# A two-layer graph attention kernel: the order inside a software-pipelined step is rearranged

## The reference, cut to what matters

```python
h = relu(layernorm(x))
s = h @ W0 @ inp.T                         # only where adj > 0
x = x + softmax(s / 0.07) @ inp            # a row without ones: the mean of inp
h = relu(layernorm(x)) @ W1
e = leaky_relu(h @ a_src [rows] + h @ a_dst [columns])
att = softmax(e where adj > 0); att below 1e-4 is dropped, the rest times the row's count of ones
x = x + elu(h + att @ h)
```

## Time and profile before

| | us |
|---|---|
| median of 3 runs | 656.26 |
| the profiled execution | 656.63 |
| its span, first to last instruction | 654.8 |
| busy: DVE | 481.7 (74%) |
| busy: ACT | 408.3 (62%) |
| busy: PE | 399.8 (61%) |
| busy: POOL | 299.5 (46%) |
| mean granted TensorE clock | 0.81 |

### The profile page before, as it was taken

How to read it: one execution, slowest core, us unless ns; L and a number is a source line. 1 busy time by engine, 2 the same in 40 slices (tenths; PEclk the granted TensorE clock), 3 DMA queues, 4 the chain that set the end, 5 groups by cost and what they waited for, 6 DMA issues and landing times.

```text
span 654.8 us, 9849 instructions
## 1 busy us (share of the span) xinstructions
PE 399.8 (61%) x3012; PEld 274.8 (42%) x3043; DVE 481.7 (74%) x2172; ACT 408.3 (62%) x424; POOL 299.5 (46%) x335
## 2 busy tenths in 40 slices
PE   2465475767668696777677765866382521546654
PEld 0111233344436263544455443635271521546653
DVE  0176178798988798979898996979847413579994
ACT  3667778999999789979889979973221100022232
POOL 6001660515151332406076674747777767777000
PEclk9657577999998889978979998867856755657777
DMA  9999999999999999999999999942222232234222
GB/s 327 413 419 421 419 368 406 383 408 407 409 408 407 370 350 392 400 407 373 367 403 369 403 398 409 397 181 55 68 70 54 71 99 53 55 103 127 75 81 83
DMA packets 37767, 186.78 MB, mean 285 GB/s; under 512 B 7888, under 2 KB 8144, under 8 KB 18896
## 3 DMA queue, kind: packets, MB, share of 16 engines
q1 hardware_dynamic: 28496, 167.02, 64.8%
q0 software_dynamic: 9216, 19.11, 10.2%
HBM read 179.73 MB, written 6.37 MB: 284 GB/s over the span
## 4 chain that ended last, share of the span: by engine, by line
DVE 41%; DMA 14%; PE 12%; POOL 11%; issue 10%; ACT 10%; SPq 2%; DVEq 0%; ACTq 0%; POOLq 0%
DMA arena<-in_adj 13%; POOL arena L808 6%; ACT arena L862 6%; PE K L1424 4%; DVE keys L1018 3%; DVE G L1129 2%; ACT R_all L891 2%; POOL X L800 2%; DVE RTp L1188 2%; POOL arena L800 2%; DVE stats L1226 1%; POOL E L808 1%; PE G L1637 1%; DVE cand L1048 1%; DVE X L1368 1%
## 5 line engine op out<-in xcount | busy, mean ns | idle before, releaser
L862 ACT ACTIVATE arena<-arena,half_c 128x2048 fp8e4<-128x2048 int32 x144 | 283.7, 1999 | 38.0 <-DMA arena<-in_adj 35.9
L800 POOL DMA_INDIRECT X<-in_L_gnn_input,idx_all x132 | 125.8, 953 | 203.9 <-DVE idx_near L1100 167.0
L1424 PE MATMUL K<-arena,bits 128*128 128x512 fp8e4 x576 | 168.0, 431 | 47.4 <-DVE keys L1018 24.2
L808 POOL DMA_INDIRECT arena<-table,idx_near x96 | 92.5, 964 | 30.3 <-issue 29.0
L1424 PEld LDWEIGHTS K<-arena,bits 128*128 128x128 bf16 x576 | 58.9, 108 | 91.1 <-ACT arena L862 28.5
L1018 DVE MAX8 keys<-K 128x8 int32<-128x128 f32 x192 | 42.4, 281 | 41.4 <-PE K L1424 41.4
L808 POOL DMA_INDIRECT E<-table,idx_near x48 | 45.6, 949 | 14.6 <-issue 14.6
L1517 PE MATMUL W<-X,RTp 128*128 128x128 f32 x240 | 35.9, 289 | 4.6 <-DVE RTp L1188 3.5
L1436 PE MATMUL G<-g,R_all 128*128 128x128 bf16 x324 | 26.5, 234 | 19.8 <-DVE g L1151 14.3
L891 ACT CAST R_all<-G 128x512 fp8e4<-128x512 f32 x36 | 19.8, 585 | 28.4 <-remote 14.9
L824 POOL TENSOR_TENSOR E<-E 128x3072 f32<-128x3072 f32 (+3 forms) x4 | 12.9, 3223 | 51.4 <-DMA E<-in_L_gnn_input 51.2
(11 more groups left out here) (255 smaller groups left out, 988.0 us busy)
## 6 DMA issues: line engine op xcount, KB each, us to landing
arena<-in_adj SPq DMA_DIRECT2D x144, 1024.0 KB, 10.8
table<-hs SPq DMA_DIRECT2D x12, 262.0 KB, 10.0
hs<-table SPq DMA_DIRECT2D x12, 262.0 KB, 2.8
E<-in_L_gnn_input SPq DMA_DIRECT2D x3, 1024.0 KB, 15.0
out_x<-x_all SPq DMA_DIRECT2D x12, 256.0 KB, 2.0
x_all<-in_x SPq DMA_DIRECT2D x1, 2560.0 KB, 14.1
X<-in_L_gnn_input,idx_all POOLq DMA_INDIRECT x132, 6.2
arena<-table,idx_near POOLq DMA_INDIRECT x96, 2.5
```

The costliest lines, as they stand in the source:

```text
L800: pool.indirect_dma_start(out=x_of(b)[:, e, :], out_offset=None, in_=inp, in_offset=bass.IndirectOffsetOnAxis(ap=idx_all[:, at:at + 1], ax ...
L808: pool.indirect_dma_start(out=E[g][:, t, :], out_offset=None, in_=tables[g], in_offset=bass.IndirectOffsetOnAxis(ap=idx_near[:, t, g:g + 1 ...
L862: nc.scalar.activation(sign[:, load % RING, :], ring[:, load % RING, :], ACT.Sign, bias=half_c[:], scale=1.0, saturate=False).then_inc(sig ...
L1424: last = mm(bank_[:], bits[:, third * TB + j, :], sign[:, load % RING, j * FOLD:(j + 1) * FOLD], start=False, stop=(third == G - 1 and j = ...
```

## The change

Four parts.

1. Order of the step. On DVE, `differences` moves from the end of a step to behind the next `decode`; `spread_lists` and `ends_of_rows` follow `list_columns` at once, ahead of `shares`; `columns_of_edges` moves ahead of `score`, `record` behind it, `norms` ahead of `centre`. On PE, `make_R`, `edges_lists` and `make_RT` move from behind the spreads to ahead of them and of the messages, `project_hid` stands between `make_R` and `edges_lists`, and six loads are folded before `edges_lists`, the last five behind the last spread. On ACT, `exponent` stands behind one load and `hidden` behind three, `keep_R` behind seven loads instead of ten, and `keep_turned_x` moves into the next step.
2. The messages (`attend`) are made in two halves of two tiles each, with three of the four spreads between them.
3. `hidden_x` of blocks 0 to 6 moves from ACT to POOL, as four operations of 128 columns and one of 512, behind the gathers of the block before.
4. `decode` loses one of its instructions per level: the exponent isn't shifted down, its weight is.

```diff
+    X_BY_POOL = 7
...
+                def hidden_x(b):
+
+                    pool.wait_ge(ln_x_r, (FROM[b] + SIZES[b] - 1) // PART + 1)
+                    wait(pool, hx_turned, b)
+                    for t in range(SIZES[b]):
+                        tile = FROM[b] + t
+                        last = pool.tensor_scalar(hx[:, t, :], x_all[:, tile, :], rstd_x[:, tile:tile + 1],
+                                                  shift_x[:, tile:tile + 1], ALU.mult, ALU.add)
+                    link(last)
+                    pool.tensor_scalar(hx[:], hx[:], 0.0, None, ALU.max).then_inc(hx_r, 1)
...
                 sum_of_input()
+                hidden_x(0)
                 EARLY = 8
                 for n in range(1, NB):
                     neighbours(n - 1, 0, BG)
+                    if n < X_BY_POOL:
+                        hidden_x(n)
...
-                        ts(exp_i[:, 0:w], code_f[:, 0:w].bitcast(I32), 23, None, ALU.logical_shift_right)
                         link(ts(top_i[:, 0:w], code_f[:, 0:w].bitcast(I32), 0x7F800000, None, ALU.bitwise_and))
-                        stt(cand[:, 0:size, level, :], exp_i[:, 0:w].rearrange("p (b e) -> p b e", b=size), float(FOLD),
-                            col_f[:, 0:w].rearrange("p (b e) -> p b e", b=size), ALU.mult, ALU.add)
+                        stt(cand[:, 0:size, level, :], top_i[:, 0:w].rearrange("p (b e) -> p b e", b=size),
+                            float(FOLD) / (1 << 23), col_f[:, 0:w].rearrange("p (b e) -> p b e", b=size), ALU.mult, ALU.add)
...
-                    pe.wait_ge(RT_r, RPARTS[b + 1])
+                    pe.wait_ge(RT_r, RPARTS[min(b + 2, NB)])
...
-                    wait(pe, rec_r, b - 2)
+                    wait(pe, rec_r, b - 3)
...
-                    wait(pe, spread_used, FROM[b])
+                    if b > 0:
+                        wait(pe, spread_used, FROM[b - 1])
...
-                def attend(b):
+                def attend(b, first, end):
...
-                    for t in range(SIZES[b]):
+                    for t in range(first, end):
...
-                    last.then_inc(att_r, 1)
+                    if end == SIZES[b]:
+                        last.then_inc(att_r, 1)
...
                     pe.wait_ge(lists_kept, min(b + 3, NB))
+                    pe.wait_ge(lists3_r, min(b + 4, NB))
```

More of the change, by code:

```diff
@@ L939, in more @@
                             convert(n, c)
+                    more(1)
                     if 0 <= b3 < NB:
                         exponent(b3)
+                    more(2)
+                    if 0 <= b4 < NB:
+                        hidden(b4)
+                    if 0 <= b2 < NB:
+                        keep_turned_x(b2)
+                    more(1)
+                    if 0 <= b3 < NB:
+                        exponent_of_edges(b3)
                     more(1)
                     if 0 <= b4 < NB:
-                        hidden(b4)
+                        keep_turned(b4)
+                    if 0 <= b2 < NB:
+                        keep_high(b2)
                     more(2)
-                    if 0 <= b3 < NB:
-                        exponent_of_edges(b3)
+                    if 0 <= b1 < NB:
+                        keep_R(b1)
                     if 0 <= b4 < NB:
-                        keep_turned(b4)
+                        keep_h(b4)
+                    more(1)
+                    if 0 <= b1 < NB:
+                        keep_RT(b1)
                     more(1)
@@ L953, in _ @@
                         hidden_x(b1)
[L954 to L965, removed]
+                    more(3)
                     if n == 0:
@@ L1247, in _ @@
                     if 0 <= b3 < NB:
-                        shares(b3)
+                        differences(b3)
                     if 0 <= b1 < NB:
                         list_columns(b1)
-                    if 0 <= b4 < NB:
-                        record(b4)
-                    if 0 <= b1 < NB:
                         spread_lists(b1)
+                        ends_of_rows(b1)
+                    if 0 <= b3 < NB:
+                        shares(b3)
+                    if n < NB:
+                        find(n, 0)
                     if 0 <= b2 < NB:
@@ L1257, in _ @@
                     if 0 <= b1 < NB:
[L1258 to L1264, removed]
+                        columns_of_edges(b1)
+                    if 0 <= b4 < NB:
+                        record(b4)
                     if n < NB:
@@ L1269, in _ @@
                         norms_of_x(0)
-                    if 0 <= b1 < NB:
-                        columns_of_edges(b1)
+                    if 0 <= b2 < NB:
+                        score(b2)
+                        pieces_of_scores(b2)
                     if 0 <= b3 < NB:
                         add_attention(b3)
-                    if 0 <= b2 < NB:
-                        centre(b2)
-                    if 0 <= b3 < NB:
                         norms(b3)
@@ L1282, in _ @@
                     if 0 <= b2 < NB:
-                        normalise(b2)
+                        rows_without_edges(b2)
+                        centre(b2)
                     if n < NB:
@@ L1286, in _ @@
                     if 0 <= b2 < NB:
-                        rows_without_edges(b2)
-                        differences(b2)
+                        normalise(b2)
                     link.step()
@@ L1560, in more @@
                             fold(n, c)
+                    more(1)
                     if 0 <= b3 < NB:
                         edge_shares(b3)
+                    more(2)
+                    if 0 <= b4 < NB:
+                        turn_hid(b4)
                     more(1)
@@ L1566, in _ @@
                         project_hx(b2)
-                    if 0 <= b4 < NB:
-                        turn_hid(b4)
+                    if 0 <= b1 < NB:
+                        first_edges(b1)
                     more(1)
+                    if 0 <= b1 < NB:
+                        make_R(b1)
                     if 0 <= b4 < NB:
                         project_hid(b4)
-                    more(2)
+                    more(1)
+                    if 0 <= b1 < NB:
+                        edges_lists(b1)
+                        make_RT(b1)
                     if 0 <= b3 < NB:
@@ L1581, in _ @@
                         spread(b2, 0)
-                    more(1)
-                    if 0 <= b2 < NB:
                         spread(b2, 1)
                         spread(b2, 2)
+                    if 0 <= b3 < NB:
+                        attend(b3, 2, SIZES[b3])
+                    if 0 <= b2 < NB:
                         spread(b2, 3)
-                    more(1)
+                    more(12)
                     if 0 <= b1 < NB:
-                        make_R(b1)
                         turn_hx(b1)
-                        edges_lists(b1)
                     if 0 <= b2 < NB:
                         rows(b2)
-                    if 0 <= b1 < NB:
-                        make_RT(b1)
-                    more(5)
                     if n == 0:
```

7 lines of the change are left out of this document (3 added, 4 removed).

## The result

The changed kernel takes 686.5 us (median of 3 runs, 686.09 to 687.44) against 656.26: ratio 1.046, 95% interval 1.0431 to 1.0486. The forecast was 676 in a range of 648 to 692. The profiled execution took 687.44, its span is 685.7.

A forecast was written before the change was run, and what follows sets the result against it. A ring of waits through ACT, PE and DVE sets the pace: 15.0 + 4.5 + 16.2 + 2.4 = 38.1 us a step against 35.8; with the tail 20 us later, 656 becomes 676, range 648 to 692.

The forecast's parts named there:

- c to `keep_R`: ACT from the last instruction of `centre` (c) through exponent, six loads, `hidden` and copies to `keep_R`: 15.0 us.
- `keep_R` to the lists: PE from `keep_R` to the lists, with `project_hid` and one fold now between: 4.5 us, bounds 1.8 and 7.
- lists to c, waits in it: DVE from the lists to the next `centre`: 16.2 us of work, plus 2.4 us of waits for PE.
- the waits at the spreads: DVE waiting for PE's spreads in the scores, before the first and fourth tiles: 1.1 and 1.3 us.
- c of step 3: Last instruction of `centre` in step 3: forecast at 160 us, 6.5 behind the unchanged kernel's 153.6.
- ring: Chain of waits through ACT, PE and DVE from one `centre` to the next: 38.1 us a step, against 35.8.
- c of step 11: Last instruction of `centre` in step 11, after eight steps of 38.1: forecast at 465 us, 25 behind 439.9.
- rival C: PE falls to its lower clock more often; half the steps 3 to 4 us longer, 692 us; chance 0.08.
- The tail: Behind the last c: POOL's rows at 507, DVE ready for the last scores at 511, finally 20 us later.
- rival A: Faster: the ring closes at 34.5 us and gathers start right behind the lists, 647 us; chance 0.23.
- The waits named: Signs: ACT idle 5 us before each exponent, DVE idle at scores and lists, DMA share 0.9, SP held by ACT.
- D: Rival: POOL computing `hidden_x` holds DVE up at their common port, 16 us more; chance 0.03.

The follow-up runs named there:

- e6: Changed kernel plus 13 unread identity products on PE in its two waits, ahead of `make_R` and of its third part: 672.69 us, ratio 1.0280.
- g1: Changed kernel with `project_hid` ahead of `first_edges`, spreads ahead of unsplit messages, `exponent` behind three loads, `keep_turned` sooner, `rows` and folds moved: 661.9 us, ratio 1.0119.
- g2: g1 with one fold ahead of the spreads, one ahead of the messages and one behind: 659.94 us, ratio 1.0094.
- e1: Changed kernel with `hidden_x` of all blocks back on ACT instead of POOL: 686.95 us, ratio 1.0490.

## Why the prediction was right, and where it was off

**The way of thinking held.** What sets the pace is the distance of two `centre`s, and each piece of it was forecast from rows of before. The time of 686.5 lies in the forecast's own band of 667 to 688, but at its edge, as the ring of 39.5 does in 37 to 39.5:

| term | predicted | measured |
|---|---|---|
| c to `keep_R` | 15.0 | 15.03 in 7 of 8 steps, 16.33 once |
| `keep_R` to the lists | 4.5 | 6.0 to 6.5 in 7 of 8, 5.5 once |
| lists to c, waits in it | 18.6 | 17.7 to 18.7 |
| the waits at the spreads | 1.1 and 1.3 | 0.5 to 1.5 and 0.93 |
| c of step 3 | 160 | 160.6 (`keep_R` 1.2 earlier than forecast, lists to c 2.2 longer) |
| ring | 38.1 | 39.5 |
| c of step 11 | 465 | 476.6 |
| time | 676 | 686.5 |

**The mis-sized term** is PE's, "I take the rows at the full clock, since most steps show it". I took the clock of before for the clock of after, though the change puts two waits, 1.49 and 1.96 us, right ahead of `project_hid`. It took 3.27 us, not 1.8, and the fold behind it 1.87, not 1.0. e6 took this alone away, and what it left are the terms of the sum, 15.03, 3.97 and 18.6: 37.6 us a step, against 38.1. That was rival C, to which I gave 0.08, and it came in nearly every step, at 1.5 to 2 us instead of 3 to 4. The piece was longer by 1.7 us on average; 0.5 of that came back, since DVE then waited less at the spreads, and 1.3 was lost once, in the step that begins at 319.05, where `first_edges` came late (c to `keep_R` 16.33). Eight times 1.4 us is 11 of the 11.6 us by which c(11) came late.

**The tail** came out nearly right by luck: three errors met. DVE was ready for the last scores at 520.71, 44.15 behind c, where I had 46.5: 2.4 us less. But POOL's rows were the later, by 3.6 us, and not DVE: they were there 47.7 behind c, where I had 42 to 43. And the 2.7 us that I added behind the last scores were 0.3. POOL in the changed kernel, in the steady state and behind it:

```profile
229.95 1.04 POOL L800 DMA_INDIRECT X<-in_L_gnn_input,idx_all  x1 [21.03 <-PE W L1534]
...
467.27 0.94 POOL L800 DMA_INDIRECT X<-in_L_gnn_input,idx_all  x1 [4.23 <-PE W L1534]
...
564.36 0.94 POOL L819 DMA_INDIRECT arena<-table,idx_near  x1 [2.05 <-DMA table<-hs]
```

I had the gathers start with the columns. They wait for the second half of the messages (L1534), whose rows they overwrite: at 229.95, though the columns were there at 223.9. It was the same before, but there the messages were done before the columns. The forecast left this wait out of POOL's sequence, and rival A with it, which would have lost a part of its gain. From the last scores to the first gather of the last third it is 40.1 us, 39.8 before.

**The waits named** were there: ACT's for `centre` (55.8 us in nine times, more than the 5 a step), DVE's for the lists (3.3 to 4.5, forecast 2, the difference being the mis-sized term again), two at the scores, a DMA share of 0.87 between 160 and 476 us (forecast 0.9), and SP held by ACT (198.7 us in 80 times between 155 and 480 us).

**The rivals.** A would have needed a ring of 34.5; even g1 and g2, with every cost found taken out, reached 35.5. D fell with e1. That part 3 is covered was right. For part 4 it is read from the slack of 1 us and more between `ends_of_rows` and `keep_R`; no run of the new order took it alone.

**Why g1 and g2 are slower than before with its ring.** Their c(11) comes 3 to 4 us later, and they are 6 to 8 us slower. The gathers' wait for the messages is not the cause, although it is there: those of block 10 start at 436.80 and 437.51, against 437.35 before, and the last scores at 493.88 and 494.28, against 494.06. The time is lost behind the last scores. Of g1_ring_short, DVE and POOL:

```profile
493.88 0.30 DVE L1146 SCALAR_TENSOR_TENSOR G<-G,arena 128x128 f32<-128x128 f32 x1 [8.46 <-DMA arena<-in_L_gnn_input,idx_all]
...
501.70 0.69 DVE L1241 TENSOR_TENSOR x_all<-x_all,K 128x512 f32<-128x512 f32 x1 [2.98 <-PE K L1533]
...
538.12 0.94 POOL L819 DMA_INDIRECT arena<-table,idx_near  x1 [5.85 <-DMA table<-hs]
```

From the last scores to the last `centre` it is 14.0 us (13.6 in g2) instead of 7.7 before, since `add_attention`, with a wait for the messages, `norms` and `rows_without_edges` stand ahead of `centre` in the new order; the first gather of the last third comes at 538.12 (537.73), against 533.90. No run moved these alone.

**What stays open.** Which limit holds the steps of the old order, the loads or DVE's own work, is argued from waits only. And the largest term of the sum, the scores between the lists and the centre, was measured but never taken out by a run.

## What to carry to other kernels

Where engines keep their order and none is full, follow one instruction from step to step, write down which engine's work and which wait lies between two of its instances, and price a moved instruction by whether it lies in that ring, on the path beside it, or outside both. Count the path beside it too: `norms` put behind `centre` gave back half of its 2.4 us there. And before moving work behind a wait, ask what holds the engine up just ahead of it: a PE that waited 1.5 and 2 us did the next products at half speed.

## What the runs showed that I had not expected

Unused products in PE's waits made the kernel faster by 12 to 14 us (686.5 to 672.7, ratio 1.0459 to 1.0280, granted clock 0.758 to 0.814). An instruction of DVE with one input, just ahead of POOL's `hidden_x`, took 0.63 us instead of 0.23, more than any with two inputs beside it lost (0.42 instead of 0.29). And exchanging two calls of the old order (f4), one that waits and one that doesn't, was worth more than the whole rearrangement: 0.6% faster against 4.6% slower.
